# Attention of a gated block: batches overlapped two deep instead of one, one maximum per step, products that run across the batch boundary

## The reference, cut to what matters

```python
q = X @ Wq.T + bq                       # 32 query heads of 16 channels
k = encoder_output @ Wk.T + bk          # 8 key groups, four heads share one
v = encoder_output @ Wv.T + bv
scores = einsum('bgrqd,bgkd->bgrqk', q, k) / sqrt(16)
scores = where(causal_mask, -inf, scores); scores = where(padding_mask, -inf, scores)
w = softmax(scores)                     # over 256 keys
out = einsum('bgrqk,bgkd->bgrqd', w, v) ...
return out @ Wo.T + bo                  # then x + tanh(gate) * this
```

## Time and profile before

| what | value |
|---|---|
| median of 3 runs | 1940.29 us |
| profiled execution | 1944.32 us, its span 1942.6 us |
| exponential of batch 0's first step | 83.6 us from the span's start |
| exponential of batch 7's first step | 550.8 us |
| PE busy over the span | 1652.5 us (85%) |

### The profile page before, as it was taken

How to read it: one execution, slowest core, us unless ns; L and a number is a source line. 1 busy time by engine, 2 the same in 40 slices (tenths; PEclk the granted TensorE clock), 3 DMA queues, 4 the chain that set the end, 5 groups by cost and what they waited for, 6 DMA issues and landing times. The chain is left out here.

```text
span 1942.6 us, 29847 instructions
## 1 busy us (share of the span) xinstructions
PE 1652.5 (85%) x11034; PEld 848.3 (44%) x11034; DVE 975.0 (50%) x1975; ACT 711.3 (37%) x1311; POOL 821.8 (42%) x853
## 2 busy tenths in 40 slices
PE   5589888877874788887799996999999999888897
PEld 3255545544542333433356653444444444343343
DVE  5465556556543577775166563346754333211136
ACT  2176667665674354544122231121111111122221
POOL 1376667666564344444144333423443342011124
PEclk9899999989986899999799997999999999999999
DMA  3531223123141444533346532735654554366655
GB/s 124 144 89 40 72 67 86 41 62 77 29 96 26 85 101 100 98 75 69 66 82 124 103 81 70 159 80 108 125 127 90 124 115 98 76 154 152 153 143 169
DMA packets 423990, 188.36 MB, mean 97 GB/s; under 512 B 365788, under 2 KB 388318, under 8 KB 423848
## 3 DMA queue, kind: packets, MB, share of 16 engines
q1 hardware_dynamic: 418168, 167.85, 38.4%
q0 software_dynamic: 5680, 18.62, 3.8%
HBM read 77.17 MB, written 22.81 MB: 51 GB/s over the span
## 5 line engine op out<-in xcount | busy, mean ns | idle before, releaser
L941 POOL TENSOR_TENSOR a_pl<-a_prob,a_ph 128x512 f16<-128x512 f32 x256 | 294.7, 1162 | 194.3 <-ACT a_prob L862 192.3
L861 ACT ACTIVATE a_ph<-bank 128x512 f16<-128x512 f32 x256 | 153.7, 600 | 148.9 <-PE bank L635 141.2
L1024 DVE TENSOR_REDUCE a_mx<-bank 128x2 f32<-128x512 f32 x256 | 165.4, 684 | 74.8 <-PE bank L617 72.3
L137 PE MATMUL bank<-XTh,d_whs 128*128 128x512 f16 x512 | 195.9, 383 | 0.9 <-ACT e_y L2295 0.7
L138 PE MATMUL bank<-XTl,d_whs 128*128 128x512 f16 x512 | 196.0, 383 | 0.0
L139 PE MATMUL bank<-XTh,d_wls 128*128 128x512 f16 x512 | 195.8, 382 | 0.0
L2133 POOL CAST d_cut<-d_raw 128x512 f16<-128x512 f32 x90 | 57.0, 634 | 239.7 <-DMA d_raw<-in_L_ffn_sw 156.2
L862 ACT ACTIVATE a_prob<-bank 128x512 f32<-128x512 f32 x256 | 154.2, 602 | 0.0
L2053 DVE TENSOR_TENSOR d_hid<-d_hid,bank 128x512 f32<-128x512 f32 x64 | 43.9, 686 | 181.5 <-PE bank L139 181.3
L1266 PE MATMUL bank<-b_wfc,b_xTh 128*128 128x512 f16 x256 | 99.5, 389 | 33.4 <-DMA b_xTl<-f_cut 25.4
L1276 PE MATMUL bank<-b_wpj,b_hTh 128*128 128x512 f16 x256 | 104.7, 409 | 21.9 <-DMA b_hTl<-b_hcut 21.8
(11 more groups left out here) (330 smaller groups left out, 4026.9 us busy)
## 6 DMA issues: line engine op xcount, KB each, us to landing
d_raw<-in_L_ffn_w SPq DMA_DIRECT2D x48, 256.0 KB, 3.1
d_raw<-in_L_ffn_sw SPq DMA_DIRECT2D x42, 256.0 KB, 3.1
made<-e_y SPq DMA_DIRECT2D x39, 256.0 KB, 2.2
a_stage<-in_L_ffn_w_fc SPq DMA_DIRECT2D x32, 256.0 KB, 2.9
a_stage<-in_L_ffn_w_proj SPq DMA_DIRECT2D x32, 256.0 KB, 3.0
a_fbuf<-in_ctx SPq DMA_DIRECT2D x16, 256.0 KB, 3.1
rows<-f_cut SPq DMA_DIRECT2D x16, 256.0 KB, 2.5
out_x<-X SPq DMA_DIRECT2D x16, 256.0 KB, 2.5
```

What stands on the lines that cost most here:

```text
L137: nc.tensor.matmul(out_ap, lhi, rhi, start=first, stop=False)
L861: nc.scalar.activation(ph[:, n % NP, :], bank[BST + n % 2][:, :], ACT.Exp)
L941: nc.gpsimd.tensor_tensor(pl[:, n % NP, :], prob[:, n % 2, :], ph[:, n % NP, :], ALU.subtract).then_inc(ev["L"], 1)
L1024: nc.vector.tensor_reduce(mx[:, tt, half, 2 * g:2 * g + 2], bank[BS + m % 2][:, :].rearrange("p (r k) -> p r k", r=2), AX_X, ALU.max)\
```

## The change

Everything is moved one batch further apart. `body(b)` now holds the main steps of batch b, one scores tile and one maximum of batch b+1 in every step, and the projections of batch b+2 (steps 10, 12, 14, 16). The front works three batches ahead.

- The 32 scores tiles are no longer ordered by token tile but by halves of the heads. The first 16 tiles need the first half of the heads alone, so turning is split too: `turn_q` and `turn_k` handle 8 transposes each, the first half of the heads of batch b+2 at steps 19 to 22 of `body(b)`, the second half at steps 0 to 3 of `body(b+1)`. Query turns use bank 6 alone and key turns bank 7 alone.
- The maxima of a half are turned by two transposes into one bank. The first half of batch b+1 goes out at step 18 of `body(b)`, the second half at step 4 of `body(b+1)`, and the main steps wait for each half by itself (`ng0` at step 0, `ng1` at step 16).
- The last three `times_v` of batch b run in steps 0 to 2 of `body(b+1)`; its last `normalise` stands at step 3, its output at steps 5, 7 and 8 instead of 11, 13 and 14. v has three buffers.
- The projections of batch 1 and half of its turning stand ahead of `body(0)`, among the scores tiles of batch 0, and so does the front of batch 2.
- The weight pieces are spread over all steps, and SP walks the 32 steps as the engines do.

```diff
-    PQ, PK = (0, 3), (1, 4)
-    TQ, TK = (6, 8), (7, 9)
-    FIRST, LAST = 10, 29
+    PQ, PK = (10, 14), (12, 16)
+    TURN0, TURN1 = 19, 0
+    NEG0, NEG1 = 18, 4
+    OTURN, OUT = 5, (7, 8)
     NORM = LAG + 8
-    OTURN, OUT = 11, (13, 14)
...
-        return m // 16, 2 * (u // 4) + u % 2, u // 2 % 2
+        return u // 8, 4 * (m // 16) + 2 * (u // 4 % 2) + u % 2, u // 2 % 2
...
             for m in range(NS):
+                if m in (2, 10):
+                    q_of(1, m // 8)
+                if m in (6, 14):
+                    kv_of(1, m // 8)
+                if m == 18:
+                    wait("lq1", 1)
+                    turn_maxima(0, 0)
+                if m in (20, 24):
+                    turn_q(1, (m - 20) // 4, 0)
+                if m in (22, 26):
+                    turn_k(1, (m - 22) // 4, 0)
                 scores(0, 0, m)
...
-                for n in range(NS + LAG):
-                    if n < NS:
-                        turned_scores(b, par, n)
+                for n in range(NS):
+                    turned_scores(b, par, n)
                     if n >= LAG:
-                        times_v(b, par, n - LAG)
+                        times_v(b, n - LAG)
+                    elif b:
+                        times_v(b - 1, NS + n - LAG)
+                    if more:
+                        scores(b + 1, 1 - par, n)
+                        if n in (TURN1, TURN1 + 2):
...
+                            turn_q(b + 1, (n - TURN1) // 2, 1)
+                        if n in (TURN1 + 1, TURN1 + 3):
...
+                            turn_k(b + 1, (n - TURN1) // 2, 1)
+                    if b and n == NEG1:
...
+                        turn_maxima(b, 1)
                     if b and n == OTURN:
...
                         turn_output(b - 1)
                     if b and n in OUT:
                         output(b - 1, OUT.index(n))
+                    if more and n == NEG0:
...
+                        turn_maxima(b + 1, 0)
...
-                    for m in due(n - 1):
-                        scores(nx, 1 - par, m)
```

More of the change, by code:

```diff
@@ new lines, in turn_k @@
+            def turn_k(b, tt, h):
+                if h == 0 and tt == 0:
+                    wait("lk0", b)
+                    wait("lk1", b)
+                    wait("lv1", b)
+                else:
+                    wait("ck", b, 2 * h + tt, 4)
+                for j in range(8):
+                    c = ks[:, tt, 4 * h + j // 2, 1 - j % 2:3 - j % 2, :].rearrange("p d c -> p (d c)")
+                    last = nc.tensor.transpose(bank16(BM + 1)[:, j * P:(j + 1) * P], c, ident16[:, :])
+                last.then_inc(ev["tk"], 1)
@@ L620, in scores, with turn_maxima @@
                 last.then_inc(ev["S"], 1)
-            def turn_maxima(b, tt):
-                wait(f"nm{tt}", b)
-                if b >= 2:
-                    wait(f"x{tt}", b - 2)
-                nc.tensor.transpose(bank16(BM + tt)[0:H0, 0:P], nmx[:, tt, :], ident16[:, :]).then_inc(ev["nt"], 1)
+            def turn_maxima(b, h):
+                wait("nm", b, h + 1, 2)
+                for tt in range(2):
+                    last = nc.tensor.transpose(bank16(BM)[0:H0 // 2, tt * P:(tt + 1) * P], nmx[:, h, tt, :], ident16[:, :])
+                last.then_inc(ev["nt"], 1)
             def turned_scores(b, par, n):
@@ L741, in body @@
                         output(b - 1, OUT.index(n))
-                    if not more:
+                    if more and n == NEG0:
+                        if more2:
+                            wait("lq1", b + 2)
+                        elif b:
+                            wait("x0", b - 1)
+                        turn_maxima(b + 1, 0)
+                    if not more2:
                         continue
@@ L847, in _, with body @@
                 high_q(0, tt)
-                high_kv(0, 0, tt)
+                high_kv(0, tt)
             normal(1, 0)
             normal(1, 1)
+            for tt in range(2):
+                high_q(1, tt)
+                high_kv(1, tt)
             take_maxima(0, 0)
+            normal(2, 0)
+            normal(2, 1)
             take_maxima(0, 1)
-            def body(b, par, more):
+            def body(b, par, more, more2):
                 for n in range(NS):
-                    if b and n == OTURN + 1:
-                        high_output(b - 1)
                     wait("ST", b, n + 1, NS)
-                    wait("AV", b, n + 1, NS)
+                    act.wait_ge(ev["AV"], b * NS + n + 1)
                     wait("L", b, n + 1, NS)
@@ L928, in _ @@
                 x_low(1, t)
+            for t in range(2):
+                ctx_high(2, t)
+                ctx_low(2, t)
             pool.wait_ge(o_in, 16)
@@ L1110, in body @@
                 for n in range(NS):
+                    if b and n == 3:
+                        normalise(old[0], b - 1, G0 // 2 - 1)
+                    if n >= NORM and (n - NORM) % 8 == 0:
+                        normalise(link, b, (n - NORM) // 8)
                     if b and n == OTURN + 1:
```

312 lines of the change are left out of this document (168 added, 144 removed).

## The result

The changed kernel takes **1861.7 us** (median of 4 runs, 1859.6 to 1870.3), beside 1942.2 us of the kernel before on the same chip: ratio 0.9599, 95% interval 0.9559 to 0.9638. The profiled execution took 1870.3 us, with a span of 1868.6.

A forecast was written before the change was run, and what follows sets the result against it. No engine was full; the ACT-POOL ring (1.28 us) would pace plain steps, PE the longer ones. Seven bodies 55.7 us less, start 9.5 more: 1944.3 to 1898.1 us profiled, 4.0 lower as median: 1894 us, range 1870 to 1925.

The forecast's parts named there:

- the side work's quarter: Full bodies: of some 13 us ACT and POOL work beside the ring, a quarter shows, 3.5 us a body.
- the pair of 2.57 us: Batch 7, before the change: two steps repeat every 2.57 us on POOL, even with weight pieces in them.
- PE's long steps: Full bodies: steps with outputs, query and key projections are set by PE, 21.1 us a body.
- the steps: Full body of 32 steps, priced one by one from PE's work and the ring: 57.0 us before side work.
- the ring: ACT's exponential and POOL's subtraction sharing two a_prob buffers: 1.28 us a plain step, whatever PE does.
- the boundary: Between batches: the 3.76 us step becomes an ordinary one, under 2 us, and PE stays at 2.4 GHz.
- the excess of batches 4 to 6: Their old 4 to 6 us over batch 2 mostly goes, since crowded weight pieces now lie about five steps apart.
- the start: Ahead of batch 0: first exponential at about 93 us instead of 83.6, 9.5 us more; x lands at about 55.6.
- Rival C: All side work hides: 57 us a body, no 1.5 us extra, 20 us less, 1874 us; chance 0.12.
- D: Rival: DVE and PE meet in every step, DVE's other work delays maxima and scores tiles; slower, 1959 us at worst; chance 0.07.
- E: Rival: steps don't level; bodies win only the boundary, 26 us, and lose it to start and late DMAs: 1940 us; chance 0.08.

The follow-up runs named there:

- e5: The changed kernel measured again, nothing altered: 1864.7 us, ratio 0.9618 to the kernel before.
- e9: Changed kernel with an extra ACT absolute value over 512 columns beside each weight piece, POOL as it was: 1885.3 us, ratio 0.9719.
- e3: Changed kernel with a batch's last three products with v back behind its own last step: 1883.8 us, ratio 0.9722.
- e14: Kernel before with the last three products run on into the next batch and DVE's last normalising moved to its fourth step: 1937.7 us, ratio 0.9998.
- e16: Changed kernel with the weight pieces' step table of the kernel before: 1868.5 us, ratio 0.9618.
- e18: Changed kernel with late scores tiles, last products behind the last step and the old pieces' table, all three undone: 1904.1 us, ratio 0.9815.
- e2: Changed kernel with the matmul that adds the mask to the second scores made twice: 1873.9 us, ratio 0.9656.
- e8: Changed kernel without the product of the probabilities' high part with v's low part, 4 of 12 small matmuls a step: 1859.8 us, ratio 0.9594.
- e6: Changed kernel with the 3 MB load of x cut in two, batch 1's piece first: 1859.7 us, ratio 0.9594.

## Why the prediction was wrong

- **Failed: the side work's quarter.** The sum charged each full body 57.0 us of steps and 3.5 us for ACT's and POOL's 13 us of side work, and batches 4 and 5 1.5 us more. These terms were 27.5 of the 411.5 us. Without them it is 384.0; measured were 385.3 (380.9 in e5). Of the 32 us between 1894 and 1861.7 the bodies are 26.2. Another 4.6 are that the profiled execution stood 8.6 us over the median and not 4.0; batch 7 and the later stages are the rest. The forecast itself named the row against its quarter, the pair of 2.57 us with pieces in it, and took it all the same. What the runs show in its place: ACT's piece in a plain pair costs nothing, a second one costs 0.53 us (e9), and POOL's low part makes step 23 of batches 0 to 3 0.8 us longer. The cost is set step by step, by what the gap still holds, and not by a share of the total. No run takes the side work of the kernel itself out. That it costs little in PE's long steps is read from the sum alone, since those steps were priced 1.8 us a body too high (next point).
- **Right: the steps.** Of the 56.9 us the groups came out as follows, forecast and measured in batch 2: steps 0 to 9 20.0 and 19.2, 10 to 17 18.2 and 17.7, 18 to 22 7.2 and 6.7, 23 to 31 11.5 and 12.4. The first three, with PE's long steps in them, came 1.8 us shorter than priced; after a long step the ring catches up, with steps of 0.95 us. The last group's 0.9 us more is step 23.
- **Right in size, incomplete in cause: the boundary.** 3.76 became 1.48 us and the clock stayed at 2.4 GHz. e3 gives 20 us to running on, with the clock falling again where it is undone. But in the old order it won nothing (e14), so it needs something else of the change, probably the maxima by halves, which the forecast did not name for it.
- **Wrong reason: the excess of batches 4 to 6.** It mostly went, as forecast. But crowded pieces alone were not its cause: their old table costs nothing in e16. What the traces show is ACT waiting, at a sign piece, for DVE's part of it. Batch 5, before and in e16:

```profile
ACT a_tern L830 <- DVE a_stage L986: 5.9, 5, 2.5
ACT a_tern L867 <- DVE a_stage L1038: 0.8, 3, 0.4
```

  In e18, with late tiles and the old table together, it is 1.6 us in batch 5. Which part of the change took this wait away is open. Batch 4 kept 4.4 us over batch 2 in the first profile and 1.4 in e5, batch 5 has less than batch 2.
- **Right: the start.** +9.5 forecast, +9.4 measured (+8.2 in e5); x landed at 54.6 us, forecast 55.6.
- **Rival C** was nearly what happened, and it was priced wrongly: its own terms take away 27.5 us and give 1866.5, not 1874. With that price the range would have had to begin lower. Its chance of 0.12 was too small beside a row that spoke for it. Batch 7 with the end of the stage (+2.5) and the later stages (-4) were not in the sum and nearly cancel.
- **D and E** fell: DVE still waits for PE 12.0 us in batch 2, and the steps did level.

## What to carry to other kernels

Where two engines hand a buffer to and fro, measure the pair's period once with and once without the side work: in those pairs, what fits into the idle part costs nothing, what goes beyond costs all of it, and a fraction in between is right only by chance. Where another engine's long step follows, part of it comes back (e9: 20 to 24 us of 33). Add or take work on one engine and compare stretches of the body, not the total alone: e2 and e8 both moved PE's long steps and left the plain ones as they were. Undo parts of a change from the changed kernel's side as well as adding them to the old one: here the parts removed cost 20 and 23 us and added up, while the same kind of part put into the old order brought nothing or lost 22 and 51 us, each behind an in-order queue that the rest of the change had also moved. And when a forecast has a case in which everything hides, add up its own terms before setting the low end.

## What the runs showed of the hardware

Two DMA transposes of x that take 1.27 us each in SyncE's queue took 3.58 and 2.02 us with the 3 MB load of x in flight ahead of them (e5), and 1.27 and 1.27 with only its first sixth ahead (e6). And four of twelve small matmuls of 0.17 us in every step, 3.2 us a body by their start-to-start distance, came out of a body with PE busy for 93% of it, and the body got only 0.6 us shorter (e8; PE's busy time fell by 1.6 us).
